# Slots of five row terms for the sampling weights, and two ScalarE copies per step in place of four

## The chip, the cores and the metric

The kernel runs on one core of a Trainium2 chip. The metric is the time of one execution on the device, in microseconds; the median of three runs of the kernel before is 2926.32 us.

## The reference, cut to what matters

The input is 32 samples of 64 channels of 56 x 56. Two residual parts follow one another. The first normalises groups, takes signs, and runs two grouped 3 x 3 convolutions with batch normalisation. The second is a deformable convolution, and the change lies in it alone:

```python
x = x + _L0_conv_ref(_gn(x), ...)
x = x + _L1_conv_ref(_gn(x), ...)

def _L1_conv_ref(x, dw_w, dw_b, om_w, om_b, vp_w, vp_b, op_w):
    value = (xf @ vp_w.T + vp_b).reshape(n, L, G, cg)           # G = 8 groups of 8 channels
    om_in = depthwise_3x3(x, dw_w) + dw_b
    om = om_in @ om_w.T + om_b                                  # 8 x 9 taps x (dy, dx, mask)
    py, px = pixel + tap + offset
    sampled = bilinear(value, py, px)                           # four neighbours, weights from the fractions
    out = einsum('nhwgk,nhwgkc->nhwgc', mask, sampled)
    return out.reshape(n, L, c) @ op_w.T
```

As long as every offset lies within one pixel, the sum over taps and neighbours touches a window of 5 x 5 pixels around the output pixel. The kernel uses that: it forms 25 window weights per pixel and group and applies them as matrix products. Other offsets raise a flag, and a general part after it does the work again; in these runs it is skipped.

## The kernel before, in words

The program has three parts: the two passes of the first block (`l0_passes`), the deformable block (`l1_pass`, line 739), and the skipped general part. The change is in `l1_pass`. It works on 16 pairs of samples, and cuts each image into 14 bands of 4 rows; one band of a pair is a step, so there are 224 steps (i is the pair, j the band). The lanes are 64 positions of a row for each of two samples.

Each engine has its own list of work per step, written out by hand, and the engines are tied by semaphores. Work for one band is spread over several steps:

- ScalarE: `hats` of step + 2 (five instructions, L1119 to L1125), every second step `copy_acc` (L1157), `copy_weights` (L1135), every second step `write_weights` (L1149, a DMA from its own queue), `taps` of step + 5 (nine products of the depthwise convolution, L1109).
- GpSimd (POOL): `merge` of step + 1 (L1062, L1065), `depthwise` of step + 4 (L1048 to L1055).
- TensorE: `apply` (L1280), `windows` (L1258), then `offsets_and_misc` (L1195, L1200, and `project`, L1207).
- VectorE: `copy_om` of step + 2 (L960, out of PSUM with the bias), `mask_hats` and `products` of step + 1 (L969, L979), in 7 of 14 steps sums for the next pair (`sum_half`, L920 to L927), and `read_misc` (L986, L952).
- SyncE issues the DMAs: values out to DRAM and back into `vbd`, window weights from DRAM into `abuf`, images in and out.

TensorE's `offsets_and_misc` waits for `read_misc` of the step before, for POOL's `depthwise` and for VectorE's `copy_om`; `copy_om` waits for the offsets of the step before; `windows` waits for POOL's `merge` and for the last `copy_weights`.

The path of the window weights is what the change touches. `copy_om` leaves the 27 x 8 offsets and masks of four rows in `oms`, with the order of the 32 values per tap as (half of the groups, row, group). `products` and `merge` keep that order in `pr`. `windows` shifts and adds them with nine matmuls per step into `win_p`, five shifts e of 160 columns, each in a place of 172 columns; a float32 matmul leaves two records in the trace. `copy_weights` spreads them into `wst` with one ScalarE instruction per row k of the band:

```python
for k in range(BR):
    to = 2 * BR * (2 - 2 * (k % 2)) + BR * u + k
```

In `wst`, a slot has 6 x 16 elements (`PC` = 96) and a lane's band 5 slots (`BAND` = 480). Two bands (u = 0, 1) share a slot. An odd row's five terms sit one place lower than an even row's, so that two rows that are neighbours can be read side by side; six places are therefore kept, and the sixth of each is zero. Every second step the whole of `wst` goes to DRAM in a skewed layout, and 14 DMAs bring it back into `abuf` so that lanes become source pixels.

`apply` multiplies the values of each source row yq (`vbd`, 32 columns of weights) with `abuf`. It takes the output rows that yq reaches, up to five, rounded outwards to pairs of rows, since pairs lie next to one another in `abuf`. Four matmuls (two samples, two halves b) stand side by side in four column tiles of the array. One half of the image width is done in even steps (34 columns, 128 lanes), the other in odd steps (26 columns, 96 lanes).

Of the kernel before, what the change touches and what calls it, by code (L numbers as in the profile page):

```python
# [30 lines left out]
S = 2  # L31
HH = H // 2
HALF = HH * W
TAPS = 9
# [10 lines left out]
G = 8  # L45
GK = G * TAPS
OMC = 3 * GK
LANES = 128
BR = 4
NT = H // BR  # L50
TN = BR * W
# [6 lines left out]
GS = 4  # L58
CT = 5
RT = 5  # L60
RP = RT + 1
WP = 172
PC = 2 * BR * RP * 2
BAND = CT * PC
PX = 4
SEEN = (PX + CT - 1) * PC
LINE = GS * SEEN + PC
QB = 36
QC = 64
VSLOT = 7  # L70
TP = 2 * W
TILES = HW // TP
# [6 lines left out]
def wait(eng, sem, value):  # L79

    if not isinstance(value, int) or value > 0:
        eng.wait_ge(sem, value)
# [656 lines left out]
def l1_pass(nc, ab3, flag, kept, w_d, v_d, out, pairs):  # L739
# [4 lines left out]
    with ctx:  # L744
        def sb(name, shape, dt=f32):
            return ctx.enter_context(nc.sbuf_tensor(name, shape, dt))
# [4 lines left out]
        def pm(name, cols):  # L751
            return ctx.enter_context(nc.psum_tensor(name, [128, cols], f32))

        N = NT * pairs
        cst, wts, ombt, vbt, smat, y, x3h = (
            kept.cst, kept.wts, kept.ombt, kept.vbt, kept.smat, kept.y, kept.x3h)
        l2h, xp, omin, vbd, eps, minus1, far = (
            kept.l2h, kept.xp, kept.omin, kept.vbd, kept.eps, kept.minus1, kept.far)
        dwt = sb("dwt", [128, 2, TAPS, TN])
        oms = sb("oms", [LANES, 2, 3 * TAPS, BR * G])  # L760
        ht = sb("ht", [LANES, 2, 3, 2 * TAPS, BR * G])
        pr = sb("pr", [LANES, 2, 11, 3, 3, BR * G])
        wst = sb("wst", [LANES, GS, BAND])
        abuf = sb("abuf", [128, S, QC * PC])
        vsb = sb("vsb", [LANES, 2, GS, G, BR * 2])
        accs = sb("accs", [128, 2, TN])
        bn3 = sb("bn3", [128, 2 * PIECES, BN_F])
# [4 lines left out]
        om_p = pm("om_p", 2 * BANK)  # L772
        win_p = pm("win_p", 2 * BANK)
        acc_p = pm("acc_p", BANK)
# [55 lines left out]
        with nc.Block() as block:  # L830
            @block.sync
            def _(sp):
# [14 lines left out]
                def read_weights(i, j, half):  # L847
# [5 lines left out]
                    for m in range(READS[half]):  # L853
                        seen = bass.AP(lines.tensor, lines.offset + (32 * half + PX * m) * LINE,
                                       [[SEEN, GS * PX], [XL * LINE, S], [1, SEEN]])
                        at = (QB * half + PX * m) * PC
                        sp.dma_start(abuf[GS * PX * m:GS * PX * (m + 1), :, at:at + SEEN], seen).then_inc(a_in[half], 16)

# [55 lines left out]
            def _(dve):  # L914
# [43 lines left out]
                def copy_om(i, j):  # L958
                    dve.wait_ge(om_ready, NT * i + j + 1)
                    dve.tensor_tensor(  # L960
                        oms[:, j % 2, :, :].rearrange("q w (b k g) -> q (w b) k g", b=2, g=GS),
                        om_p[:, :].rearrange("q (k z) -> q k z", k=BR)[:, :, 0:OMC].rearrange("q k (v g) -> q v k g", g=GS),
                        ombt[:, :].rearrange("q (v g) -> q v g", g=GS).unsqueeze(2).broadcast_to([LANES, 6 * TAPS, BR, GS]),
                        ALU.add).then_inc(om_ok, 1)

                def mask_hats(i, j):
# [53 lines left out]
                for j in range(2):  # L1020
                    copy_om(0, j)
# [70 lines left out]
            def _(act):  # L1092
# [34 lines left out]
                def copy_weights(i, j):  # L1127
                    t, u = NT * i + j, j % 2
                    if u == 0:
                        wait(act, w_out, 16 * (t // 2))  # L1130
                    act.wait_ge(win_ok, t + 1)
                    for k in range(BR):
                        to = 2 * BR * (2 - 2 * (k % 2)) + BR * u + k
                        cells = wst[:, 0, to:to + 1]
                        ins = act.activation(  # L1135
                            bass.AP(cells.tensor, cells.offset, [cells.ap[0], [PC, CT], [2 * BR, 2 * RT], [BAND, GS]]),
                            win_p[:, 0:CT * WP].rearrange("p (e z) -> p e z", e=CT)[:, :, 0:RT * BR * G].rearrange(
                                "p e (m k g) -> p e m k g", k=BR, g=GS)[:, :, :, k, :],
                            ACT.Copy)
                    ins.then_inc(wst_ok, 1)  # L1140

                def write_weights(i, j):
# [3 lines left out]
                    for half in range(2):  # L1146
                        wait(act, a_in[half], 16 * READS[half] * (D - 1))
                    lines = w_d[D % 2, :].rearrange("(l z) -> l z", z=LINE)[:, 0:GS * SEEN].rearrange("l (g q) -> l g q", q=SEEN)
                    act.dma_start(lines[:, :, 0:BAND], wst[:, :, :]).then_inc(w_out, 16)  # L1149

# [35 lines left out]
            def _(pe):  # L1186
# [63 lines left out]
                def windows(i, j):  # L1250
                    t = NT * i + j
                    wait(pe, wst_ok, t)
                    pe.wait_ge(mg_ok, t + 1)
                    for e in range(CT):
                        terms = [(a, b) for a in range(3) for b in range(3) if 2 - (a + b - 2) == e]
                        to = WP * e
                        for n, (a, b) in enumerate(terms):
                            mm = pe.matmul(win_p[:, to:to + 160], smat[:, e, :],  # L1258
                                           pr[:, j % 2, 0:RT, a, b, :],
                                           start=n == 0, stop=n == len(terms) - 1)  # L1260
                    mm.then_inc(win_ok, 1)

                def apply(i, j, half):

                    D, y0 = (NT * i + j) // 2, BR * j
                    pe.wait_ge(a_in[half], 16 * READS[half] * (D + 1))
                    if half == 0:
                        for b in range(j + 1 if j else 0, min(j + 3, NT)):
                            pe.wait_ge(vb_in[b % VSLOT], 4 * 16 * (2 * i + b // VSLOT + 1))
                        wait(pe, accs_ok, D)  # L1270
                    qb, K, x0, x1 = ((0, 128, 0, 34), (1, 96, 30, W))[half]
                    rows = range(max(0, y0 - 2), min(H, y0 + 2 * BR + 2))
                    for yq in rows:
                        t0, t1 = max(0, yq - y0 - 2) // 2, min(2 * BR - 1, yq - y0 + 2) // 2
                        for s in range(S):
                            for b in range(2):
                                seen = abuf[0:K, s, :]
                                at = (QB * qb + x0 - 32 * qb + 2) * PC + 4 * BR * (y0 + 2 * t0 - yq + 3) + 2 * BR * b + 2 * t0
                                mov = bass.AP(seen.tensor, seen.offset + at, [seen.ap[0], [8 * BR + 2, t1 - t0 + 1], [PC, x1 - x0], [1, 2]])
                                mm = pe.matmul(  # L1280
                                    acc_p[32 * (2 * s + b):32 * (2 * s + b) + 32, 0:2 * TN].rearrange("p (t w r) -> p t w r", t=BR, r=2)[:, t0:t1 + 1, x0:x1, :],
                                    vbd[0:K, 1 - s, qb, yq // BR % VSLOT, :, :, 2 * (yq % BR) + b].rearrange("p g c -> p (g c)"),
                                    mov, start=yq == rows[0] and qb == 0, stop=yq == rows[-1] and qb == 1,
                                    skip_group_check=True)
                    mm.then_inc(amat_ok, 1)

                def step(i, j, first, last):
# [15 lines left out]
                for j in range(LAG):  # L1303
                    if j < 4:
                        apply(pairs - 1, NT - 4 + j // 2 * 2, j % 2)
                    offsets_and_misc(N + j + 3, output=(pairs - 1, NT + j - LAG))
# [275 lines left out]
def program(nc, x, w1t, w2t, par, con, con3, wts3, omb, vpb, places, out):  # L1582

    samples = x.shape[0]
    pairs = samples // S
    l1_d = nc.dram_tensor("l1_scratch", [pairs, 128, HALF], f32).ap()
    l2_d = nc.dram_tensor("l2_scratch", [pairs, S * CO, HW], f32).ap()
    x3_d = nc.dram_tensor("x3_scratch", [samples, C, HW], f32).ap()
    w_d = nc.dram_tensor("weight_scratch", [2, LANES * LINE], f32).ap()
    v_d = nc.dram_tensor("rows_scratch", [2, LANES * BR * C], f32).ap()  # L1590
    vpad = nc.dram_tensor("value_scratch", [G * VP * VP, C // G], f32).ap()
    with nc.sbuf_tensor("ab3", [128, 2], f32) as ab3, nc.sbuf_tensor("flag", [1, 1], i32) as flag:
        with ExitStack() as ctx:
            kept = Kept(nc, ctx, x, x3_d, l2_d, con3, wts3, omb, vpb, pairs)
            l0_passes(nc, x, w1t, w2t, par, con, l1_d, l2_d, x3_d, ab3, kept, pairs)
            l1_pass(nc, ab3, flag, kept, w_d, v_d, out, pairs)
        l2_s = l2_d.rearrange("q (s c) f -> (q s) c f", s=S)
        general_pass(nc, x, x3_d, l2_s, ab3, flag, con3, wts3, omb, vpb, places, vpad, out, samples)
# [66 lines left out]
```

## Time and profile before

| | us |
|---|---|
| median of 3 runs | 2926.32 |
| lowest, highest of the runs | 2924.11, 2930.4 |
| the profiled execution | 2924.83 |
| its span, from the first to the last instruction | 2923.0 |
| PE busy (matmuls) | 2430.8 |
| PE weight loads busy | 2021.2 |
| DVE busy | 2205.6 |
| ACT busy | 2259.7 |
| POOL busy | 1917.6 |

The span covers all parts of the program; the deformable block begins after some 700 us. Busy times are sums over the whole span, and a matmul's end is modelled, so a busy TensorE need not be at its peak. The waits name what ended an engine's idle time, as far as the profile shows it; "issue" stands where it shows nothing. The mean time of an instruction counts its latency, and successive ones overlap, so busy time by count is shorter.

### The profile page before, as it was taken

The numbers are of one execution on the slowest core, as the hardware profiler recorded it, in microseconds if no ns is written. First come the engines' busy times: TensorE is split into PE (matmuls) and PEld (weight loads), VectorE is DVE, ScalarE is ACT, GpSimd is POOL, SyncE is SP. The second block draws the span as 40 slices with busy tenths as digits, with TensorE's granted clock in tenths as the row PEclk, the third lists the DMA queues.
The fourth block names the chain that finished last, engine by engine and source line by source line (L and its number), as shares of the span: only waits on it lengthen the run. The fifth ranks groups of instructions, "written<-read, shape, count | busy, mean of one in ns | idle before, by whom it ended". The sixth has DMA issues, their size and how long they took to land. (4 is left out here: it accounts for less than half of the span.)

```text
span 2923.0 us, 100581 instructions
## 1 busy us (share of the span) xinstructions
PE 2430.8 (83%) x40456; PEld 2021.2 (69%) x40456; DVE 2205.6 (75%) x3095; ACT 2259.7 (77%) x4721; POOL 1917.6 (66%) x1452
## 2 busy tenths in 40 slices
PE   3999779993688888888888888888888888888887
PEld 2666556772577777777777777777777777777786
DVE  3555423334989897989888898989898988989773
ACT  2444256662989889898989898898989898989892
POOL 1000000003888888888988888888988898988892
PEclk8999889996899999999999999999999999999998
DMA  4555579975577677777777777777778777877675
GB/s 103 130 132 144 143 182 265 263 199 172 124 191 203 181 195 192 188 191 190 204 194 192 187 200 195 197 183 193 199 189 198 188 196 187 206 179 190 177 176 147
DMA packets 356164, 538.18 MB, mean 184 GB/s; under 512 B 171728, under 2 KB 258256, under 8 KB 355536
## 3 DMA queue, kind: packets, MB, share of 16 engines
q1 hardware_dynamic: 296656, 422.71, 60.3%
q10 hardware_dynamic: 59136, 110.11, 10.8%
q8 instruction: 283, 4.64, 0.8%
q14 instruction: 89, 0.73, 0.1%
HBM read 312.82 MB, written 219.77 MB: 182 GB/s over the span
## 5 line engine op out<-in xcount | busy, mean ns | idle before, releaser
L1109 ACT ACTIVATE dwt<-xp,wts 128x224 f32<-128x224 f32 x2016 | 797.3, 484 | 40.8 <-ACT wst L1135 31.8
L1280 PE MATMUL acc_p<-abuf,vbd 128*32 128x136 f32 (+5 forms) x20480 | 710.4, 291 | 54.9 <-issue 46.0
L1280 PEld LDWEIGHTS acc_p<-abuf,vbd 128*32 128x32 f32 (+1 forms) x20480 | 645.9, 145 | 117.7 <-issue 60.5
L979 DVE TENSOR_TENSOR pr<-mh_p,ht 128x864 f32<-128x864 f32 x672 | 668.9, 1051 | 23.2
L1258 PE MATMUL win_p<-pr,smat 128*128 128x160 f32 x4032 | 626.7, 310 | 27.3 <-POOL pr L1065 15.8
L246 PE MATMUL cv<-cin,wb 128*64 128x392 bf16 x6912 | 590.4, 333 | 25.8 <-ACT cin L225 25.8
L1258 PEld LDWEIGHTS win_p<-pr,smat 128*128 128x128 f32 x4032 | 570.4, 194 | 51.2 <-issue 22.4
L246 PEld LDWEIGHTS cv<-cin,wb 128*64 128x64 bf16 x6912 | 401.4, 110 | 208.7 <-ACT cin L225 25.9
L1048 POOL TENSOR_TENSOR dwt<-dwt 128x896 f32<-128x896 f32 x224 | 516.3, 2305 | 4.7 <-ACT dwt L1109 4.7
L1062 POOL TENSOR_TENSOR pr<-pr 128x576 f32<-128x576 f32 x224 | 317.3, 1417 | 187.8 <-DVE pr L979 187.8
L1135 ACT ACTIVATE wst<-win_p 128x200 f32<-128x200 f32 x896 | 388.6, 605 | 62.4 <-PE win_p L1258 38.7
L969 DVE TENSOR_TENSOR mh_p<-oms,ht 128x864 f32<-128x864 f32 x224 | 408.8, 1825 | 8.5 <-ACT ht L1125 8.5
L1200 PE MATMUL om_p<-wts,omin 64*64 64x216 f32 x3584 | 406.4, 369 | 10.2 <-POOL omin L1055 10.2
L1195 PE MATMUL misc<-wts,xp 64*64 64x64 f32 x3584 | 181.6, 234 | 265.7 <-issue 214.3
L1195 PEld LDWEIGHTS misc<-wts,xp 64*64 64x64 f32 x3584 | 149.8, 137 | 311.2 <-issue 310.7
L1065 POOL TENSOR_TENSOR pr<-pr 128x576 f32<-128x576 f32 x224 | 338.7, 1512 | 31.2
L1050 POOL TENSOR_TENSOR dwt<-dwt 128x448 f32<-128x448 f32 x224 | 336.5, 1502 | 17.6
L1200 PEld LDWEIGHTS om_p<-wts,omin 64*64 64x64 f32 x3584 | 246.1, 139 | 47.8 <-issue 11.6
L986 DVE TENSOR_TENSOR y<-y,misc 128x224 f32 (+1 forms) x224 | 85.2, 380 | 248.2 <-PE misc L1207 247.5
L253 ACT ACTIVATE lt<-cv 128x392 f32<-128x392 f32 x128 | 60.9, 492 | 265.9 <-PE cv L246 265.5
L960 DVE TENSOR_TENSOR oms<-om_p,ombt 128x864 f32<-128x864 f32 x224 | 238.2, 1063 | 10.1 <-PE om_p L1200 10.1
L1119 ACT ACTIVATE ht<-oms 128x576 f32<-128x576 f32 x224 | 151.2, 675 | 102.7 <-DVE oms L960 102.4
(132 smaller groups left out, 2674.9 us busy)
## 6 DMA issues: line engine op xcount, KB each, us to landing
abuf<-weight_scratch SPq DMA_DIRECT2D x1568, 96.0 KB, 3.3
weight_scratch<-wst ACTq DMA_DIRECT2D x112, 960.0 KB, 6.2
xt<-x SPq DMA_DIRECT2D x128, 392.0 KB, 7.6
rows_scratch<-vsb SPq DMA_DIRECT2D x224, 128.0 KB, 2.1
vbd<-rows_scratch SPq DMA_DIRECT2D x896, 32.0 KB, 3.2
x_scratch<-xt SPq DMA_DIRECT2D x64, 392.0 KB, 6.6
y<-x SPq DMA_DIRECT2D x64, 392.0 KB, 4.4
x3h<-x_scratch SPq DMA_DIRECT2D x64, 392.0 KB, 4.9
```

Of the source, the lines that this page charges most:

```text
L246: mm = pe.matmul(cv[c][64 * h:64 * h + 64, 0:CN], wb[:, layer, j, k, :], cin[:, u, r:r + CR, k % 3:k % 3 + W], start=(k == 0 and j == 0), ...
L969: dve.tensor_tensor(mh[:, :, :, :], oms[:, j % 2, 2 * TAPS:3 * TAPS, :].unsqueeze(1).broadcast_to([LANES, 3, TAPS, BR * G]), ht[:, j % 2, ...
L979: dve.tensor_tensor(pr[:, j % 2, slots, :, :, :].rearrange("p k e x z -> p e k (x z)"), mh[:, a, :, :].rearrange("p (k x) z -> p k (x z)", ...
L1048: pool.tensor_tensor(d[:, 0:4, :], d[:, 0:4, :], d[:, 4:8, :], ALU.add).then_inc(dw1_ok, 1)
L1050: pool.tensor_tensor(d[:, 0:2, :], d[:, 0:2, :], d[:, 2:4, :], ALU.add).then_inc(dw2_ok, 1)
L1065: pool.tensor_tensor(rows(slice(1, 3)), rows(slice(1, 3)), rows(slice(5, 11, 5)), ALU.add).then_inc(mg_ok, 1)
L1109: ins = act.activation(dwt[:, j % 2, k, :].rearrange("p (r w) -> p r w", w=W), image[:, r:r + BR, k % 3:k % 3 + W], ACT.Identity, scale=dw ...
L1135: ins = act.activation(bass.AP(cells.tensor, cells.offset, [cells.ap[0], [PC, CT], [2 * BR, 2 * RT], [BAND, GS]]), win_p[:, 0:CT * WP].rea ...
L1195: return pe.matmul(misc[64 - 64 * s:128 - 64 * s, to:to + C], xp[64 * s:64 * s + 64, at:at + XL], vpw[64 * s:64 * s + 64, :], start=True, ...
L1200: return pe.matmul(om_p[64 * s:64 * s + 64, 256 * r:256 * r + OMC], omin[64 * s:64 * s + 64, j % 2, r, :], omw[64 * s:64 * s + 64, :], sta ...
L1258: mm = pe.matmul(win_p[:, to:to + 160], smat[:, e, :], pr[:, j % 2, 0:RT, a, b, :], start=n == 0, stop=n == len(terms) - 1)
L1280: mm = pe.matmul(acc_p[32 * (2 * s + b):32 * (2 * s + b) + 32, 0:2 * TN].rearrange("p (t w r) -> p t w r", t=BR, r=2)[:, t0:t1 + 1, x0:x1, :],
```

## The change

A slot gets five places of 16 elements (`PC` = 80). An odd row's first term, which lay in the place that only odd rows used, now lies in the last place of the slot before it, which odd rows leave free; one more place ends a band (`BAND` = 416). `SEEN`, `LINE`, `QB`, `QC` and the size of `abuf` follow from that.

`copy_weights` writes with one instruction per parity r of the row. It takes two rows k of the same parity as its innermost pair, 8 bytes apart in `wst`, and 400 elements. For the source to be read at an even step, the order of the 32 values per tap becomes (group, row): `copy_om` reads `om_p` with the four rows innermost, which lie 256 elements apart in PSUM, and still writes `oms` without a gap. `win_p` loses its padding; its fourth shift now crosses the end of a bank of 512 columns, and its matmuls are cut into 32 and 128 columns.

In `apply`, pairs can no longer be padded with zeros at the ends, since the neighbouring place holds another slot's term. A source row is applied in up to three runs: an odd first row alone, the pairs, and an even last row alone.

```diff
-RP = RT + 1
-WP = 172
-PC = 2 * BR * RP * 2
-BAND = CT * PC
+RW = 4 * BR
+PC = RT * RW
+BAND = CT * PC + RW
 PX = 4
-SEEN = (PX + CT - 1) * PC
+SEEN = (PX - 1) * PC + BAND
 LINE = GS * SEEN + PC
-QB = 36
-QC = 64
+QB = 37
+QC = 65
...
-        abuf = sb("abuf", [128, S, QC * PC])
+        abuf = sb("abuf", [128, S, QC * PC + RW])
...
                     dve.tensor_tensor(
-                        oms[:, j % 2, :, :].rearrange("q w (b k g) -> q (w b) k g", b=2, g=GS),
-                        om_p[:, :].rearrange("q (k z) -> q k z", k=BR)[:, :, 0:OMC].rearrange("q k (v g) -> q v k g", g=GS),
-                        ombt[:, :].rearrange("q (v g) -> q v g", g=GS).unsqueeze(2).broadcast_to([LANES, 6 * TAPS, BR, GS]),
+                        oms[:, j % 2, :, :].rearrange("q w (g k) -> q (w g) k", k=BR),
+                        om_p[:, :].rearrange("q (k z) -> q z k", k=BR)[:, 0:OMC, :],
+                        ombt[:, :].unsqueeze(2).broadcast_to([LANES, OMC, BR]),
                         ALU.add).then_inc(om_ok, 1)
...
-                    for k in range(BR):
-                        to = 2 * BR * (2 - 2 * (k % 2)) + BR * u + k
+                    for r in range(2):
+                        to = RW * (1 - r) + BR * u + r
                         cells = wst[:, 0, to:to + 1]
                         ins = act.activation(
-                            bass.AP(cells.tensor, cells.offset, [cells.ap[0], [PC, CT], [2 * BR, 2 * RT], [BAND, GS]]),
-                            win_p[:, 0:CT * WP].rearrange("p (e z) -> p e z", e=CT)[:, :, 0:RT * BR * G].rearrange(
-                                "p e (m k g) -> p e m k g", k=BR, g=GS)[:, :, :, k, :],
+                            bass.AP(cells.tensor, cells.offset, [cells.ap[0], [2 * BR, 2 * CT * RT], [BAND, GS], [2, 2]]),
+                            win_p[:, 0:CT * RT * BR * G].rearrange("p (m g k r) -> p r m g k", g=GS, k=2, r=2)[:, r],
                             ACT.Copy)
...
-                        to = WP * e
+                        cuts = (0, 1, RT) if e == 3 else (0, RT)
                         for n, (a, b) in enumerate(terms):
-                            mm = pe.matmul(win_p[:, to:to + 160], smat[:, e, :],
-                                           pr[:, j % 2, 0:RT, a, b, :],
-                                           start=n == 0, stop=n == len(terms) - 1)
+                            for m0, m1 in zip(cuts, cuts[1:]):
+                                mm = pe.matmul(win_p[:, BR * G * (RT * e + m0):BR * G * (RT * e + m1)], smat[:, e, :],
+                                               pr[:, j % 2, m0:m1, a, b, :],
+                                               start=n == 0, stop=n == len(terms) - 1)
...
-                        t0, t1 = max(0, yq - y0 - 2) // 2, min(2 * BR - 1, yq - y0 + 2) // 2
...
+                        k0, k1 = max(0, yq - y0 - 2), min(2 * BR - 1, yq - y0 + 2)
+                        t0, t1 = (k0 + 1) // 2, (k1 + 1) // 2
+                        runs = (((k0, 1, 1),) if k0 % 2 else ()) + (((2 * t0, t1 - t0, 2),) if t1 > t0 else ()) + (
+                            ((k1, 1, 1),) if k1 % 2 == 0 else ())
+                        for ka, n, r in runs:
...
+                                    row = y0 + ka - yq + 3 - ka % 2
+                                    at = (QB * qb + x0 - 32 * qb + 2) * PC + RW * row + 2 * BR * b + ka
+                                    mov = bass.AP(seen.tensor, seen.offset + at, [seen.ap[0], [2 * RW + 2, n], [PC, x1 - x0], [1, r]])
+                                    mm = pe.matmul(
+                                        acc_p[32 * (2 * s + b):32 * (2 * s + b) + 32, 0:2 * TN].rearrange("p (t w r) -> p t w r", t=BR, r=2)[
+                                            :, ka // 2:ka // 2 + n, x0:x1, ka % 2:ka % 2 + r],
```

## Rows read from the trace of the kernel before

**Rows 1.** Busy time by stretch, 1200 to 2800 us: from:to, length, engines, PEclk, DMA share, GB/s

```profile
core 0: us, PE busy (x) PEld busy (x) DVE busy (x) ACT busy (x) POOL busy (x), PEclk, DMA share, GB/s
1200.00:2800.00 1600.00, 1345.38 (x24810) 1186.20 (x24804) 1416.43 (x1800) 1436.87 (x3273) 1390.53 (x1031) 0.97 0.76 191
```

**Rows 2.** Groups by line, same stretch, DVE: xcount | busy us, mean ns | idle before

```profile
L960 DVE TENSOR_TENSOR oms<-om_p,ombt 128x864 f32<-128x864 f32 x166 | 176.5, 1063 | 0.0
...
L952 DVE TENSOR_TENSOR vsb<-misc,vbt 128x128 f32<-128x128 f32 x332 | 112.2, 430 | 0.0
...
L986 DVE TENSOR_TENSOR y<-y,misc 128x224 f32 (+1 forms) x166 | 63.1, 380 | 153.9 <-PE misc L1207 153.3
```

**Rows 3.** Waits, same stretch: engine, line, waited for: us, times, longest

```profile
PE misc L1195 <- issue: 161.9, 113, 3.0
DVE y L986 <- PE misc L1207: 153.3, 75, 5.9
POOL pr L1062 <- DVE pr L979: 134.8, 87, 6.1
ACT ht L1119 <- DVE oms L960: 78.1, 32, 6.3
...
PE misc L1195 <- DVE oms L960: 35.2, 12, 4.5
...
ACT wst L1135 <- DMA weight_scratch<-wst: 17.7, 15, 2.1
...
PE misc L1207 <- ACT accs L1157: 7.8, 12, 1.2
```

**Rows 4.** Timeline, 1717 to 1731 us: start, length, instruction, [idle before]

```profile
1725.81 2.99 DVE L979 TENSOR_TENSOR pr<-mh_p,ht 128x864 f32<-128x864 f32 x3
...
1726.36 0.66 POOL L1055 TENSOR_TENSOR omin<-dwt 128x224 f32<-128x224 f32 x1
...
1727.23 0.27 PE L1195 MATMUL misc<-wts,xp 64*64 64x64 f32 x2 [2.11 <-issue]
...
1727.91 1.41 POOL L1062 TENSOR_TENSOR pr<-pr 128x576 f32<-128x576 f32 x1 [0.89 <-DVE pr L979]
...
1728.76 0.59 PE L1207 MATMUL misc<-accs,wts 64*64 64x112 f32 x8
...
1729.50 0.39 DVE L986 TENSOR_TENSOR y<-y,misc 128x224 f32 x1 [0.70 <-PE misc L1207]
...
1730.31 1.06 DVE L960 TENSOR_TENSOR oms<-om_p,ombt 128x864 f32<-128x864 f32 x1
```

**Rows 5.** Groups by line, whole span, ACT

```profile
L1135 ACT ACTIVATE wst<-win_p 128x200 f32<-128x200 f32 x896 | 388.6, 605 | 62.4 <-PE win_p L1258 38.7 <-DMA weight_scratch<-wst 23.5
...
L1119 ACT ACTIVATE ht<-oms 128x576 f32<-128x576 f32 x224 | 151.2, 675 | 102.7 <-DVE oms L960 102.4
...
L225 ACT ACTIVATE cin<-xt 64x1568 bf16 (+1 forms) x64 | 96.8, 1512 | 2.0
...
L253 ACT ACTIVATE lt<-cv 128x392 f32<-128x392 f32 x128 | 60.9, 492 | 265.9 <-PE cv L246 265.5
L1157 ACT ACTIVATE accs<-acc_p 128x448 f32<-128x448 f32 x112 | 59.0, 527 | 27.2 <-PE acc_p L1280 27.1
```

**Rows 6.** Groups by line, whole span, PE

```profile
L1280 PE MATMUL acc_p<-abuf,vbd 128*32 128x136 f32 (+5 forms) x20480 | 710.4, 291 | 54.9 <-issue 46.0 <-DMA abuf<-weight_scratch 8.6
...
L1189 PE MATMUL misc<-rh,cst 128*128 128x2 f32 x32 | 7.9, 317 | 17.9 <-DVE rh L937 17.9
```

**Rows 7.** Timeline of PE, four blocks of matmuls in different steps

```profile
1729.28 2.55 PE L1280 MATMUL acc_p<-abuf,vbd 96*32 96x104 f32 x80
...
1781.12 3.42 PE L1280 MATMUL acc_p<-abuf,vbd 128*32 128x68 f32 x96
...
2017.98 2.79 PE L1280 MATMUL acc_p<-abuf,vbd 96*32 96x52 f32 x96
2020.70 2.71 PE L1258 MATMUL win_p<-pr,smat 128*128 128x160 f32 x18
```

**Rows 8.** DMA queues of the page: packets, MB, share of 16 engines

```profile
q8 instruction: 283, 4.64, 0.8%
```

More of the change, by code:

```diff
@@ L1273, in apply @@
                     for yq in rows:
-                        t0, t1 = max(0, yq - y0 - 2) // 2, min(2 * BR - 1, yq - y0 + 2) // 2
[L1275 to L1284, printed above, removed]
+                        k0, k1 = max(0, yq - y0 - 2), min(2 * BR - 1, yq - y0 + 2)
@@ new lines, in apply @@
+                        t0, t1 = (k0 + 1) // 2, (k1 + 1) // 2
+                        runs = (((k0, 1, 1),) if k0 % 2 else ()) + (((2 * t0, t1 - t0, 2),) if t1 > t0 else ()) + (
+                            ((k1, 1, 1),) if k1 % 2 == 0 else ())
+                        for ka, n, r in runs:
+                            opens = qb == 0 and yq == rows[0] and ka == k0
+                            for s in range(S):
+                                for b in range(2):
+                                    seen = abuf[0:K, s, :]
+                                    row = y0 + ka - yq + 3 - ka % 2
[4 more added lines that the diff above has]
+                                            :, ka // 2:ka // 2 + n, x0:x1, ka % 2:ka % 2 + r],
+                                        vbd[0:K, 1 - s, qb, yq // BR % VSLOT, :, :, 2 * (yq % BR) + b].rearrange("p g c -> p (g c)"),
+                                        mov, start=opens, stop=yq == rows[-1] and qb == 1 and ka == runs[-1][0],
+                                        skip_group_check=True)
```

## The prediction

> **What bounds the kernel now.** I read the busy times of the steady stretch first, then who waited for whom in it, then one turn of the loop in the timeline, then the rows that price single instructions.
>
> Between 1200 and 2800 us no engine is full: ACT 1437, DVE 1416, POOL 1391 and PE 1345 us of 1600 [rows 1]. The third part runs 166 of its 224 steps there, one `copy_om` (L960) each [rows 2], so a step takes 1600 / 166 = 9.64 us. A loop sets the pace, and the waits show which [rows 3]. POOL waits 134.8 us for DVE's products. DVE waits 153.3 us for PE's `misc`. PE waits 161.9 us ahead of `misc`, in 113 steps, put down to "issue". The timeline tells what that is [rows 4]: POOL's `omin` ends at 1726.36 + 0.66 = 1727.02, and PE, idle for 2.11 us, starts at 1727.23. So it is DVE products, POOL merge and depthwise, PE offsets and `misc`, DVE addition and `copy_om`, and round again. `copy_om` (L960) stands in that loop; the ScalarE copies do not. ACT is the busiest engine, but what others wait for on it in 1600 us is 7.8 us of `accs` [rows 3].
>
> **The change part by part.**
>
> *ScalarE copies.* ACT's slope from the two SBUF rows is (1512 - 675) / (1568 - 576) = 0.844 ns per element, so a copy out of PSUM has 492 - 392 x 0.844 = 161 ns fixed [rows 5]. `accs` reads PSUM at a step of two elements and fits that: 161 + 378 = 539 against 527. The old copy, 200 elements in 605 ns, pays (605 - 161) / 200 = 2.22 ns per element: the price is in the write, where each element lands 1920 bytes from the last. Four of them cost 4 x 434 (388.6 / 896) = 1.74 us per step, successive ones overlapping by 605 - 434 = 171 ns. A new copy of 400 writes two cells 8 bytes apart, then jumps. Low end, no jump is paid: 499 ns each, 0.83 us for two with the overlap. High end, every element is still paid: 1049 ns, 1.93 us. If two share a jump, 1.53 ns each, it is 1.38 us. I take 1.1, between the low end and the shared jump: 0.63 us saved, 141 us of ACT over 224 steps. The Trainium skill, in Advanced Engine Details and Errata, section Memory Cachelines, says that SBUF lines are 16 bytes and that two hits on a line absorb its latency; by that it would be the low end, 0.83. No row here has two hits per line.
>
> What of it reaches the end is bounded by the waits on ACT: 7.8 us in 1600, so 7.8 x 224 / 166 = 11 us. I take -10. Below that nothing waits; a ScalarE that is done earlier waits longer for `oms` (78.1 us already, in 32 steps [rows 3]).
>
> *`copy_om`.* Same count, same contiguous write, but its PSUM read now takes four elements 1 KB apart before it moves on, where it took four neighbours. DVE's rows: slope (1063 - 380) / (864 - 224) = 1.07 ns per element, 140 ns fixed [rows 2]. It already runs at that slope, so there is nothing to gain. Upper end: what DVE pays for a scattered SBUF write, `vsb`, (430 - 140) / 128 = 2.27 ns per element; 864 at that price are 2.10 us, 1.04 us more per step, on the loop. I take 0: the nearest row, ACT's `accs`, steps over every second PSUM element and pays nothing [rows 5]. The upper end is the first rival.
>
> *Windows on PE.* Their outputs now stand without padding, so the fourth shift would cross column 512 (the code's BANK), and its two terms are cut into 32 and 128 columns: 22 matmul records per step for 18. Columns are the same. Low end: 0. High end: the row with short matmuls on 128 x 128 weights, L1189, 7.9 / 32 = 247 ns each [rows 6], so 4 x 0.25 = 1.0 us. 18 records of 160 columns take 2.71 us [rows 7], 0.15 each; a 32-column record streams a fifth of that but still loads all 128 weight columns. I take 0.075 us for each added one, 0.30 per step, nearer to the stream than to L1189, whose matmuls wait for nothing behind them.
>
> *Apply on PE.* Before: 12 source rows inside an image, each as one run of one to three row pairs for four side-by-side tiles, two passes: 96 records per half. After, odd ends are runs of one row: 8 single rows, 4 single pairs, 6 double pairs, 18 runs, 144 records; columns fall from 48 to 40 rows' worth. In the 26-wide half, 96 records take 2.79 us and 80, without two one-pair runs, 2.55 [rows 7]: 0.24 / 4 = 60 ns per pass of a single pair. Less a last matmul's 0.25 us, 2.54 - 8 x 0.060 = 2.06 us are left for 40 pairs in longer runs, 51 ns each. After: 8 x 60 + 24 x 51 + 16 singles. A single costs 26 ns if only columns count and 60 if the pass has a floor: 2.12 to 2.66 us, -0.42 to +0.12. The 34-wide half (3.42 us), worked alike with 66 ns a pair, gives -0.5 to 0. I take the upper ends, since a lone pair of 52 columns is dearer than one in a run: +0.06 per step on average. A single also writes every second PSUM element; twice the column price, 52, is still under the 60.
>
> *Instructions.* PE's matmul records go from 40456 to 52104 (20480 x 122 / 80 in apply, 4032 x 22 / 18 in windows). Instructions come by DMA, 283 packets [rows 8]; PE's idle time put down to issue inside apply is 46.0 us [rows 6]. If it grows with apply's records, +52%, that is 24 us.
>
> *PE on the path.* (0.30 + 0.06) x 224 + 24 = 105 us. PE waits ahead of `misc` in 113 + 12 of 166 steps [rows 3]; in the other 41, a quarter, added work delays `misc`. In 7 of 14 steps DVE is then still busy with the next image's sums. 105 x 0.25 x 0.5 = 13 us; at least 0, at most 26.
>
> *DMA, SP, POOL.* A slot is 320 bytes for 384, so the weight write falls from 960 to 832 KB and each read from 96 to 82. Counts and queues stay. The one wait it eases is ACT's 17.7 us for the write [rows 3], and ACT is off the loop: 0. SP gets no new wait. POOL's clears shrink before the loop starts: 0.
>
> **Sum.** -10 + 13 + 0 = +3 on the profiled 2924.83 us, whose span is 2923.0; that execution is 1.5 us under the median of the runs, so the forecast is 2929 us. About 0.2%, 6 us, is what a measurement can tell from no change.
>
> **The rivals.**
>
> 1. *`copy_om` pays for its scattered PSUM read.* Slower. 1.04 us more on the loop's one DVE entry, with ACT's hats, DVE's mask and PE's next offsets queued behind it. DVE waits for `misc` in 75 of 166 steps [rows 3]; if those hid it, 0.55 x 224 x 1.04 = 128 us would remain, if none did, 233. As the wait itself is a return of the same loop I take 150: 3076 us. It decides once an element costs more than some 0.05 ns extra. For it: DVE does pay double for scattered writes. Against: `accs`. Chance 0.22. The Trainium skill, same section, gives PSUM lines of 8 bytes and says "Every two consecutive elements should be contiguous for best throughput", which would make this rival true; by the same rule `accs`, one element per line, should be slow, and it is not.
>
> 2. *PE becomes the bound.* Lone rows above the 60 ns, windows near 1 us, or instruction fetch that no longer keeps up with shorter instructions; with 1.3 us more per step PE's 1345 us become 1560 of 1600. Half of the excess over its waits, some 25 us, shows: 2952 us. For it: the idle times at issue. Against: 161.9 us of waiting. Chance 0.17.
>
> 3. *ACT sets the pace after all.* It waits for `oms` in 32 and for PE in a few of 166 steps and runs through in most. If taps that come 0.63 us earlier pull POOL's depthwise forward in a third of the steps, 0.33 x 224 x 0.63 = 47, some 35 after what PE gives back: 2891 us. Against: POOL shows no wait for taps in the stretch. Chance 0.14.
>
> 4. *The copies do not get cheaper.* The jump is paid per element, 1.93 us for 1.74; ACT loses 0.2 per step and some of its slack: 2933 us. Chance 0.05.
>
> **How the numbers follow.** The forecast has 0.42, with a range of its own of 2912 to 2945: of it 0.08 lies under 2920, 0.24 within 6 us, 0.10 above. Faster: 0.08 + 0.14 = 0.22. Same: 0.24 + 0.02 + 0.03 from rivals 2 and 4 = 0.29. Slower: 0.10 + 0.22 + 0.15 + 0.02 = 0.49. The range for 8 in 10 reaches from rival 3, 2890, to rival 1, 3085; it leaves out rival 1's upper end.
>
> **What the new profile would show.** L1135's successor at some 600 to 700 ns for 400 elements, two per step; `copy_om` at 1.06 us (2.1 makes rival 1); windows near 3.0 us per step and apply within 0.2 of 2.8 and 3.4 us; DVE's wait for `misc` near 150 us, ACT's for `oms` well above 78.1. I am wrong on the loop if ACT's waits stay small while the time falls, and on PE if its wait ahead of `misc` vanishes.

## The result and the profile after

The changed kernel takes 2987.86 us (median of 4 runs, 2986.08 to 2995.11) against 2925.22 us for the kernel before on the same chip: ratio 1.022, 95% interval 1.0193 to 1.0246. It is slower by some 63 us; whether by more or less than 2%, the interval leaves open. The profiled execution took 2987.32 us, its span 2985.5. The granted clock is 0.945 over its span and was 0.952 before. It is not what is looked for: a run below with 0.931 takes about as long (2991.37 us, though with fewer columns), and the same instructions in another order, also below, keep PE busy for 2534.6 us at 0.953, only 11 us less than here (2545.8).

First the pace. In 1200 to 2800 us, busy time by stretch and VectorE's group `copy_om` of the changed kernel, the answers to [rows 1, 2]:

```profile
1200.00:2800.00 1600.00, 1384.18 (x32182) 1250.44 (x32175) 1351.88 (x1754) 1282.15 (x2838) 1328.44 (x994) 0.95 0.60 170
```

```profile
L959 DVE TENSOR_TENSOR oms<-om_p,ombt 128x864 f32<-128x864 f32 x160 | 171.8, 1074 | 0.0
```

160 steps stand where 166 stood: 10.0 us each for 9.64. Six steps of 9.64 us are 58 us lost in this stretch, known to about one step. No engine is full: PE has 1384 of 1600 us, only 39 more than before. So it is not PE's busy time that became the bound. The waits of the same stretch, which answer to [rows 3]:

```profile
DVE y L985 <- PE misc L1205: 217.2, 73, 7.3
POOL pr L1061 <- DVE pr L978: 199.7, 105, 5.3
...
ACT wst L1134 <- PE win_p L1257: 130.2, 61, 5.3
PE acc_p L1285 <- issue: 128.6, 82, 4.5
ACT ht L1118 <- DVE oms L959: 126.9, 49, 6.2
...
PE misc L1193 <- issue: 56.9, 56, 2.5
```

and two rows of the kernel before, same view, that weren't shown:

```profile
PE acc_p L1280 <- issue: 38.0, 32, 3.2
...
ACT wst L1135 <- PE win_p L1258: 21.7, 14, 4.3
```

Everybody now waits longer for PE: VectorE for `misc` (153.3 to 217.2 us), ScalarE for the windows (21.7 to 130.2), and POOL behind VectorE (134.8 to 199.7). PE itself waits much less for the others (ahead of `misc` 161.9 to 56.9 us). It stands still inside `apply`, where no other engine and no data hold it: 38.0 to 128.6 us. The groups by line over the whole span, against [rows 2, 5, 6]:

```profile
L1257 PE MATMUL win_p<-pr,smat 128*128 128x160 f32 (+2 forms) x4928 | 755.5, 313 | 33.3 <-issue 20.0 <-POOL pr L1064 13.3
L1285 PE MATMUL acc_p<-abuf,vbd 128*32 128x34 f32 (+5 forms) x31232 | 726.7, 251 | 177.3 <-issue 173.1 <-DMA abuf<-weight_scratch 4.2
...
L959 DVE TENSOR_TENSOR oms<-om_p,ombt 128x864 f32<-128x864 f32 x224 | 240.2, 1072 | 11.6 <-PE om_p L1198 11.6
L1134 ACT ACTIVATE wst<-win_p 128x400 f32<-128x400 f32 x448 | 216.8, 543 | 205.9 <-PE win_p L1257 194.8 <-DMA weight_scratch<-wst 10.5
```

The copies do what the change wants: two of 543 ns for four of 605. `copy_om` is unchanged. `apply` is busy 16 us longer, and idle at issue 173.1 us for 46.0: 127 us more. In the timeline of PE such a pause looks like this (the last two rows are a step without one):

```profile
2005.17 2.68 PE L1285 MATMUL acc_p<-abuf,vbd 96*32 96x26 f32 x128
2008.91 0.45 PE L1285 MATMUL acc_p<-abuf,vbd 96*32 96x52 f32 x16 [1.07 <-issue]
```

```profile
1723.87 2.91 PE L1285 MATMUL acc_p<-abuf,vbd 96*32 96x26 f32 x144
1726.71 3.06 PE L1257 MATMUL win_p<-pr,smat 128*128 128x160 f32 x22
```

`apply` has no wait on a semaphore between its 1st and 144th record. The queue of [rows 8] grew in step:

```profile
q8 instruction: 374, 6.13, 0.9%
```

That is 91 packets more. A matmul record has a weight load beside it, so PE has 2 x (52104 - 40456) = 23296 instructions more: 256 per added packet. I numbered PE's instructions in the order of the trace (a record two, with its load; the sequencer's own one each) and took every pause of over 450 ns between two loads of one line after 1000 us. All 111 of the changed kernel stand at number 156 or 157 modulo 256; so do all 46 of the kernel before. And between 1200 and 2800 us such a pause ends 1.3 to 1.6 us after the end of an instruction packet's transfer (10th to 90th percentile; before 1.3 to 1.7). PE stands at the border of two packets and waits for the second one. The Trainium skill has this in Advanced Engine Details and Errata, section ISA Cache: a line holds 256 instructions, and there are two lines. (The same lines give TensorE 128 KB, which at 16 KB a line would be eight.) The trace agrees with 256 instructions, 16 KB a packet, and with one line in hand while the next one comes: none of the 254 packets of this stretch sets out more than 294 instructions ahead of its border. Their median is 143 instructions ahead, but the 93 that PE then waits for have a median of 80; before it was 42 of 197 packets, with a median of 80 as well. Busier DMA engines are not the reason: their share fell from 0.76 [rows 1] to 0.60.

### The profile page after: what moved, and what is told of

It reads as the page before. It is cut to its first block and busy times, and to the rows that moved or that the text cites. A ratio compares the mean times of both kernels' runs of the same rounds, so it can differ in the third digit from the quotient of the medians.

```text
span 2985.5 us, 123429 instructions
## 1 busy us (share of the span) xinstructions
PE 2545.8 (85%) x52104; PEld 2169.7 (73%) x52104; DVE 2172.3 (73%) x3095; ACT 2112.7 (71%) x4273; POOL 1899.9 (64%) x1452
## 5 line engine op out<-in xcount | busy, mean ns | idle before, releaser
L1285 PE MATMUL acc_p<-abuf,vbd 128*32 128x34 f32 (+5 forms) x31232 | 726.7, 251 | 177.3 <-issue 173.1
L1285 PEld LDWEIGHTS acc_p<-abuf,vbd 128*32 128x32 f32 (+1 forms) x31232 | 680.6, 155 | 227.0 <-issue 191.9
L1257 PE MATMUL win_p<-pr,smat 128*128 128x160 f32 (+2 forms) x4928 | 755.5, 313 | 33.3 <-issue 20.0
L1257 PEld LDWEIGHTS win_p<-pr,smat 128*128 128x128 f32 x4928 | 699.1, 206 | 49.5 <-issue 25.7
L1198 PE MATMUL om_p<-wts,omin 64*64 64x216 f32 x3584 | 393.9, 361 | 8.7 <-POOL omin L1054 8.6
L968 DVE TENSOR_TENSOR mh_p<-oms,ht 128x864 f32<-128x864 f32 x224 | 375.3, 1675 | 7.1 <-ACT ht L1124 7.1
L1134 ACT ACTIVATE wst<-win_p 128x400 f32<-128x400 f32 x448 | 216.8, 543 | 205.9 <-PE win_p L1257 194.8
L1049 POOL TENSOR_TENSOR dwt<-dwt 128x448 f32<-128x448 f32 x224 | 321.3, 1434 | 17.6
L1198 PEld LDWEIGHTS om_p<-wts,omin 64*64 64x64 f32 x3584 | 239.6, 137 | 44.9 <-issue 10.6
L959 DVE TENSOR_TENSOR oms<-om_p,ombt 128x864 f32<-128x864 f32 x224 | 240.2, 1072 | 11.6 <-PE om_p L1198 11.6
```

The lines of the kernel that those rows point to most:

```text
L968: dve.tensor_tensor(mh[:, :, :, :], oms[:, j % 2, 2 * TAPS:3 * TAPS, :].unsqueeze(1).broadcast_to([LANES, 3, TAPS, BR * G]), ht[:, j % 2, ...
L1049: pool.tensor_tensor(d[:, 0:2, :], d[:, 0:2, :], d[:, 2:4, :], ALU.add).then_inc(dw2_ok, 1)
L1198: return pe.matmul(om_p[64 * s:64 * s + 64, 256 * r:256 * r + OMC], omin[64 * s:64 * s + 64, j % 2, r, :], omw[64 * s:64 * s + 64, :], sta ...
L1257: mm = pe.matmul(win_p[:, BR * G * (RT * e + m0):BR * G * (RT * e + m1)], smat[:, e, :], pr[:, j % 2, m0:m1, a, b, :], start=n == 0, stop= ...
L1285: mm = pe.matmul(acc_p[32 * (2 * s + b):32 * (2 * s + b) + 32, 0:2 * TN].rearrange("p (t w r) -> p t w r", t=BR, r=2)[:, ka // 2:ka // 2 + ...
```

## The experiments

Theory A: the split runs of `apply` ask for instructions faster than they come, and the pauses are the loss. 288 instructions in 2.91 us are 10.1 ns each, so a packet's 256 last 2.6 us, where they lasted 3.7 (192 in 2.79 us [rows 7]). From a packet's start to the end of a pause go 2.3 to 2.9 us (10th to 90th percentile; before 2.4 to 3.3). Rivals: B, the four added window matmuls; C, the slots and their reads; D, the lone rows' own columns.

**The split alone, on the old slots.**

```diff
-    t0, t1 = max(0, yq - y0 - 2) // 2, min(2 * BR - 1, yq - y0 + 2) // 2
...
+    for ka, n, r in runs:
...
+    at = (QB * qb + x0 - 32 * qb + 2) * PC + 4 * BR * (y0 + ka - ka % 2 - yq + 3) + 2 * BR * b + ka
```

> The kernel before with nothing changed but apply, which issues the same runs as the changed kernel (odd ends of a source row as runs of one row, 144 matmul records per half for 96) on the old six-place slots. Theory A (more and shorter matmuls in apply outrun the supply of PE's instructions): idle at issue inside apply rises from 46 us to 150 to 190 over the whole span, and the time from 2925 to 2970 to 2990 us. Rival B (the four added window matmuls are what costs): at most 2940 us. Rival C (the five-place slots, their reads at other addresses and the later reads of them): 2925 to 2935 us.

2996.74 us, ratio 1.0237 (1.0206 to 1.0267). `apply` of that kernel, groups by line:

```profile
L1285 PE MATMUL acc_p<-abuf,vbd 128*32 128x34 f32 (+5 forms) x31232 | 771.3, 260 | 186.3 <-issue 178.7 <-DMA abuf<-weight_scratch 7.2
```

The split alone brings the whole loss, with the pauses (178.7 us) that were expected; the time is 7 us above the expected range. As causes of the loss, B and C fall.

**All but the split.**

```diff
-    for ka, n, r in runs:
...
+    t0, t1 = max(0, yq - y0 - 2) // 2, min(2 * BR - 1, yq - y0 + 2) // 2
+    at = (QB * qb + x0 - 32 * qb + 2) * PC + RW * (y0 + 2 * t0 - yq + 3) + 2 * BR * b + 2 * t0
```

> The changed kernel with apply's runs as before (whole row pairs, 96 records per half) on the five-place slots; the odd end of a run then reads the neighbour of its pair, which belongs to another slot, so apply's sums are not the reference's. Everything else of the change stays: copies, copy_om order, cut windows, smaller slots. Theory A: 2910 to 2935 us, idle at issue inside apply back at 40 to 60 us over the span. Rival B or C: 2960 us or more.

2917.51 us, ratio 0.9969 (0.9957 to 0.9982):

```profile
L1279 PE MATMUL acc_p<-abuf,vbd 128*32 128x136 f32 (+5 forms) x20480 | 658.1, 280 | 52.6 <-issue 48.4 <-DMA abuf<-weight_scratch 3.7
...
L1134 ACT ACTIVATE wst<-win_p 128x400 f32<-128x400 f32 x448 | 215.7, 540 | 99.4 <-PE win_p L1257 90.2 <-DMA weight_scratch<-wst 8.4
```

The pauses are back at 48.4 us and the rest of the change is worth some 10 us to the good. The busy time of 658.1 us for the same records that took 710.4 [rows 6] is taken up below.

**Count or columns.**

```diff
     for ka, n, r in runs:
+        xe = x1 if r == 2 else x0 + 2
...
```

(`xe` then takes the place of `x1` in what is read and in what is written.)

> The changed kernel with the runs of one row cut to 2 of their 26 or 34 columns (that work is left out); the count of matmuls stays. Theory A (count of instructions): 2970 to 2995 us, idle at issue inside apply 160 to 230 us, since PE asks for instructions sooner still. Rival D (the lone rows' own columns, with every second PSUM element written, are what costs): 2935 us or less.

2991.37 us, ratio 1.0218 (1.0196 to 1.024); waits in 1200 to 2800 us:

```profile
PE acc_p L1286 <- issue: 129.1, 66, 4.1
```

With 2 columns for 26 or 34 in every lone row the kernel takes as long as the changed one. D falls: it is the count of instructions. This is the run with the granted clock of 0.931.

**The windows' cut alone.**

```diff
+    cuts = (0, 1, RT) if e == 3 else (0, RT)
+    for m0, m1 in zip(cuts, cuts[1:]):
         for n, (a, b) in enumerate(terms):
-            mm = pe.matmul(win_p[:, to:to + 160], ...)
+            mm = pe.matmul(win_p[:, WP * e + BR * G * m0:WP * e + BR * G * m1], ...)
```

> The kernel before with the fourth shift's windows cut into 32 and 128 columns, as in the changed kernel, and nothing else: 22 matmul records per step for 18. Windows take 3.0 to 3.1 us per step for 2.71. Theory A: that alone is small beside the loss, 2926 to 2940 us, with the idle time at issue inside apply within 15 us of the 38 in 1200 to 2800 us. Rival B: 2960 us or more.

2935.61 us, ratio 1.0033 (1.0017 to 1.0048), some 9.5 us. The two parts of the cut run one after the other here, where the changed kernel alternates them. `apply`, groups by line:

```profile
L1281 PE MATMUL acc_p<-abuf,vbd 128*32 128x136 f32 (+5 forms) x20480 | 703.3, 289 | 54.1 <-issue 43.9 <-DMA abuf<-weight_scratch 9.9
```

Idle time at issue in `apply` is about as before. So the cut has a small price of its own, inside the expected range, and B is excluded a second time.

**The copies alone.** The old slots can take two copies, with the loops in another order and `copy_om` as it was:

```diff
-    for k in range(BR):
-        to = 2 * BR * (2 - 2 * (k % 2)) + BR * u + k
+    for r in range(2):
+        to = 4 * BR * (1 - r) + BR * u + r
...
+            bass.AP(cells.tensor, cells.offset, [cells.ap[0], [BAND, GS], [PC, CT], [2 * BR, 2 * RT], [2, 2]]),
+            bass.AP(taken.tensor, taken.offset, [taken.ap[0], [1, GS], [WP, CT], [4 * GS, 2 * RT], [2 * GS, 2]]),
```

> The kernel before with nothing changed but the ScalarE copies: two of 400 elements that write neighbours, on the old six-place slots, with windows, apply and copy_om as they were. If the write alone decides (theory A takes it so), a copy takes 500 to 560 ns although it now reads PSUM at a step of eight elements, two per step of the loop; the time is 2905 to 2925 us, since PE's instructions are what they were. If the copies' earlier end were itself harmful (rival E: other cores' work of the loop collides with earlier windows), 2940 us or more.

2934.71 us, ratio 1.0025 (1.0014 to 1.0036): slower, against theory A's 2905 to 2925, and short of rival E's 2940. Groups by line:

```profile
L1279 PE MATMUL acc_p<-abuf,vbd 128*32 128x136 f32 (+5 forms) x20480 | 702.4, 290 | 73.5 <-issue 66.9 <-DMA abuf<-weight_scratch 6.4
...
L1257 PE MATMUL win_p<-pr,smat 128*128 128x160 f32 x4032 | 645.0, 316 | 42.9 <-issue 26.0 <-POOL pr L1065 16.8
...
L1135 ACT ACTIVATE wst<-win_p 128x400 f32<-128x400 f32 x448 | 211.6, 530 | 122.6 <-PE win_p L1257 107.9 <-DMA weight_scratch<-wst 14.3
```

The windows of the kernel before, same view:

```profile
L1258 PE MATMUL win_p<-pr,smat 128*128 128x160 f32 x4032 | 626.7, 310 | 27.3 <-POOL pr L1065 15.8 <-issue 10.7 <-ACT wst L1135 0.6
```

The copy is as cheap as expected, but with PE's program unchanged its pauses grew (46.0 to 66.9 us in `apply`, 10.7 to 26.0 in the windows). Why they grew is open. It is tempting to say that PE's idle time ahead of `misc` let the next packet come, and that a faster ScalarE shortens it; the trace does not bear that out. Between 1200 and 2800 us, 1 of the 197 packets of the kernel before sets out while PE waits there (197 us; 24 packets by share of time), and 0 of 196 with the copies alone (174 us). If the pauses ate the gain, it must appear once they are gone.

**The same instructions in another order.** Eight of the twelve source rows, then the windows, then the other four; first on the changed kernel, then on the kernel before, then on the copies alone:

```diff
-    for yq in rows:
+    for yq in (rows[0:8], rows[8:])[part]:
...
-    apply(*n, j % 2)
+    apply(*n, j % 2, 0)
     windows(i, j)
+    if n:
+        apply(*n, j % 2, 1)
```

> The changed kernel with the order of PE's work alone altered: eight of apply's source rows, then the windows, then the other four rows, and the offsets after them. Every instruction stays, so 374 instruction packets stay. Theory A, put as density (288 instructions in some 2.9 us are asked for faster than one packet of 256 comes, 2.3 to 2.9 us; the windows' 44 slow ones in between let the next packet arrive): idle at issue inside apply falls from 177 us over the span to under 70, the time to 2925 to 2955 us. Rival F (each added packet costs, wherever it falls): 2975 to 2995 us. Against both: accs are ready later, so PE may wait for them ahead of the projection, up to 1 us in every second step.

> The kernel before with the same reordering (eight source rows, windows, four rows) and nothing else. By theory A it had 46 us of such idle time inside apply over the span; if that shrinks to under 20 and the wait for accs stays small, 2895 to 2925 us. If what PE waits for ahead of misc is what sets the pace and the idle time lay beside it, 2920 to 2932 us. If the later accs cost more than the supply gives back, 2940 us or more.

> The kernel with the copies alone (two of 400, old slots, old runs) and the same reordering. The copies alone came out 7 us slower than before while the idle time at issue inside apply rose by some 17 us in the 1600 us looked at; by theory A the reordering takes that away and leaves the copies' gain: 2885 to 2920 us, below both others. If the copies cost something of their own, it stays 5 us or more above the kernel before with the reordering.

| us (ratio, interval) | old order | eight and four |
|---|---|---|
| changed kernel | 2987.86 (1.022) | 2934.06 (1.0023, 1.0011 to 1.0036) |
| kernel before | 1 | 2915.45 (0.996, 0.9945 to 0.9975) |
| copies alone | 2934.71 (1.0025) | 2908.65 (0.9936, 0.9914 to 0.9959) |

`apply` in the three, groups by line, in this order (one fence per kernel):

```profile
L1286 PE MATMUL acc_p<-abuf,vbd 128*32 128x34 f32 (+5 forms) x31232 | 754.4, 252 | 73.6 <-issue 54.1 <-DMA abuf<-weight_scratch 19.3
```

```profile
L1281 PE MATMUL acc_p<-abuf,vbd 128*32 128x136 f32 (+5 forms) x20480 | 742.5, 292 | 29.5 <-DMA abuf<-weight_scratch 29.0
```

```profile
L1280 PE MATMUL acc_p<-abuf,vbd 128*32 128x136 f32 (+5 forms) x20480 | 744.7, 292 | 24.4 <-DMA abuf<-weight_scratch 23.3 <-issue 0.8
```

The changed kernel gives back 54 of its 63 us with 374 packets as before, so F (each packet costs, wherever it falls) is wrong: by theory A, what costs is that they are wanted in a bunch. The kernel before gives back about 11 us of time with its 46.0 us of pauses. And with the pauses gone the copies alone are 6.8 us faster than the kernel without them, where they had been 7 us slower: the gain is real, and the old order hid it. The new order does a second thing, though. ScalarE gets its windows sooner, and waits 34.5 us for them in the changed kernel where it waited 194.8:

```profile
L1134 ACT ACTIVATE wst<-win_p 128x400 f32<-128x400 f32 x448 | 215.0, 540 | 34.7 <-PE win_p L1257 34.5
```

That is rival G below, and no reordered run has the one without the other.

**Six and six, and windows first.** `rows[0:6]` and `rows[6:]` on the changed kernel and on the copies alone; `rows[0:0]` and all of `rows` on the changed kernel.

> The changed kernel with apply's source rows in two halves of six around the windows, where eight and four left 54 us of idle time at issue inside apply over the span. Theory A (density: at most 144 apply instructions, 1.5 us, come one after the other for 192, 2 us): under 25 us of it, and 2910 to 2928 us, on a level with or below the kernel before. If the remaining loss is the 12 longer bursts' place and not their length, or the later accs cost as much, it stays at 2930 us or more.

> The copies alone with six and six rows for eight and four. With eight and four its idle time at issue inside apply was 0.8 us, so theory A has nothing left to give: 2904 to 2914 us, at most 4 us from the 2908.65. Later accs would show as 2915 us or more.

> The changed kernel with the windows wholly ahead of apply, so that the ScalarE copies get theirs sooner still but all 288 instructions of apply stand together. Theory A (the density of apply is what costs): idle at issue inside apply stays at 100 us or more over the span and the time at 2960 us or more. Rival G (what the reordering mended is that windows came too late for ScalarE): 2940 us or less whatever the idle time is. PE may also wait for POOL's merge ahead of the windows, up to 2 us per step, which apply covered before; a high time with a low idle time at issue would be that and would tell nothing.

The changed kernel comes to 2918.14 us (0.9958, 0.9944 to 0.9973), its pauses in `apply` to 12.1 us (first fence); the copies alone to 2903.79 us (0.9917, 0.9901 to 0.9934), a little below what was expected and the fastest version here. The second fence has ScalarE's copies in that one, and what they wait for:

```profile
L1286 PE MATMUL acc_p<-abuf,vbd 128*32 128x136 f32 (+5 forms) x31232 | 752.1, 252 | 41.5 <-DMA abuf<-weight_scratch 28.5 <-issue 12.1
```

```profile
L1135 ACT ACTIVATE wst<-win_p 128x400 f32<-128x400 f32 x448 | 209.5, 526 | 9.7 <-DMA weight_scratch<-wst 5.8 <-PE win_p L1257 3.9
```

With the windows wholly ahead the changed kernel took 2939.32 us (1.0035, 1.0022 to 1.0049). Theory A's expectation of it was wrong, and by its letter G's (2940 us or less) came true. PE's groups there:

```profile
L1257 PE MATMUL win_p<-pr,smat 128*128 128x160 f32 (+2 forms) x4928 | 718.2, 304 | 210.4 <-POOL pr L1064 182.8 <-DMA abuf<-weight_scratch 25.5 <-ACT wst L1134 1.0
L1286 PE MATMUL acc_p<-abuf,vbd 128*32 128x34 f32 (+5 forms) x31232 | 696.5, 249 | 23.4 <-issue 18.0 <-DMA abuf<-weight_scratch 4.5
```

288 instructions stand together, and yet the pauses are 18.0 us, not 100. So the density of `apply` by itself does not decide; what goes before it counts. Here 44 slow instructions (3.03 us) and a wait for POOL's merge go before, and when a packet sets out some 120 or more instructions of the one before it are still to be done in nine of ten cases; in the changed kernel one packet in ten has 2 or fewer. That is counted from the trace, but which of the two, the slow matmuls or the wait, gives the packet its lead was not taken apart; only 1 of 261 packets sets out during that wait. Nor does this run tell A from G, since its pauses went as well. Against G as the whole account stands the kernel with whole runs: ScalarE waits 90.2 us for windows there, for 38.7 before [rows 5], and yet it is 10 us faster, though its copies are shorter too. That the split costs, and that PE's added idle time lies at the borders of packets, is shown; how much of what the new order gives back is due to the packets, and how much to the earlier windows, is not.

## Why the prediction was wrong

The forecast of 2929 us (own range 2912 to 2945) was wrong; the second rival happened, in the third of its forms, at more than twice its price (63 us for some 25). "Slower" had the largest chance, and the range for 8 in 10 holds the result, but that is luck: the upper part of the range and 0.22 of the 0.49 were there for the first rival, which is false.

- **The step that failed** is the term for instructions, "If it grows with apply's records, +52%, that is 24 us". Measured: +127 us, 46.0 to 173.1. The idle time does not grow with the records. A pause is what a packet takes less what the instructions in hand last, and inside `apply` 256 of them last 2.6 us for 3.7. The packets that PE waits for set out with some 80 instructions in hand; those last 0.8 us for 1.2 before (10.1 for 14.5 ns each), and a packet takes 2.3 to 2.9. In the stretch the pauses inside `apply` are longer, 1.6 us for 1.2 on average, and above all more, 82 for 32; what decides when a packet sets out, and so how many are late, no run explains. The packets were there [rows 8], and so were the times per block [rows 7]; I divided neither by the other, and did not ask how long a packet takes.
- **PE on the path** ("105 x 0.25 x 0.5 = 13 us") failed with it. Half of the added idle time reached the end: 63 us of 127, about the share that I gave to rival 2 and not to the forecast. (Rival 2's "some 25" is for the 1600 us; over 224 steps it would be 36.) The cover, the waits ahead of `misc` in 125 of 166 steps, was largely used up: 61 of 160 are left.
- **The rival's reason against itself**, "161.9 us of waiting", didn't hold: 105 of these went.
- **ScalarE copies**: predicted 1.1 us per step with a low end of 0.83; two take 216.8 / 224 = 0.97. The overlap of 171 ns was taken off four times for the old copies and once for the new pair; taken off twice, the low end is 0.66, the shared jump 1.20, and rival 4 pays 1.76 for 1.74. The Trainium skill's rule on two hits per line (Advanced Engine Details and Errata, section Memory Cachelines), which was named for the low end, is nearly borne out: 543 ns for 400 elements where 200 took 605, that is 0.96 ns per element above the 161 ns for 2.22 before, where SBUF rows give 0.844. What reaches the end was put at 10 us; it measures 6.8 with the pauses gone (2915.45 to 2908.65) and -7 with them.
- **`copy_om`**: 1072 ns for 1063. Right; the first rival, which had the larger chance, is false for this read. The Trainium skill's sentence on PSUM pairs (same page and section), which the prediction took to make it true, stands there beside one on matmuls; for this VectorE read it is not borne out.
- **Windows**: +0.30 us per step predicted; 3.06 for 2.71 measured. By the prediction's own factors that is 0.30 x 224 x 0.125 = 8.4 us, and the cut alone cost 9.5. Right.
- **Apply's busy time**: +0.06 per step (13 us) predicted, +16 us measured, by two errors that cancel. Single undisturbed blocks in the timeline, first of the split on old slots, then of whole runs on new slots:

```profile
1824.09 3.04 PE L1285 MATMUL acc_p<-abuf,vbd 96*32 96x26 f32 x144
...
1850.79 3.53 PE L1285 MATMUL acc_p<-abuf,vbd 128*32 128x34 f32 x144
```

```profile
1825.66 2.59 PE L1279 MATMUL acc_p<-abuf,vbd 96*32 96x52 f32 x96
...
1952.30 3.15 PE L1279 MATMUL acc_p<-abuf,vbd 128*32 128x68 f32 x96
```

The medians of all blocks without a gap (no matmul starts over 250 ns after the last), at a granted clock of 1, are 2.78 and 3.43 us before, 3.05 and 3.57 with the split, 2.62 and 3.18 on the new slots: the split costs 0.27 and 0.14 us, the new slots save 0.16 and 0.25.
- **DMA**: 0, and ScalarE's wait for the write was to ease: 17.7 to 8.2 us in the stretch. Nothing of the loss lies there.

The sign named for an error on PE ("if its wait ahead of `misc` vanishes") is what the waits show.

## What to carry to other kernels

Where an engine's program is unrolled, count its instructions per microsecond in the densest stretch and hold that against the rate at which its packets come, before costing an edit by columns: here 256 instructions in 2.6 us were too many and in 3.7 us mostly not. It is a warning and not a rule: with the windows wholly ahead the same dense block had few pauses. Idle time at issue inside a block without semaphores is the sign, and a changed order (slow matmuls between the fast ones) took it away here without one instruction less. An edit that is worth little may be hiding behind such pauses, and should be tried again once they are gone.

## What was not expected of the hardware

- Every pause of PE inside a block stands at a border of 256 instructions (111 of 111, 46 of 46). The same program of PE had 66.9 us of them in `apply` for 46.0 once the copies were cheaper.
- While PE waits for other engines, hardly any instruction packet sets out: ahead of `misc`, 1 of 197 in 197 us before, 0 of 254 in 67 us in the changed kernel, where the share of time would make it 24 and 11. So such a wait helps only a packet that is already under way.
- The same matmuls on `abuf` ran 6 to 7% faster with slots 320 bytes apart than with 384 (medians 2.62 for 2.78 us, 3.18 for 3.43). The copies alone and the cut alone leave them at 2.78 and 3.42. What does it, the size of the step, where it falls in memory, or the smaller DMA traffic beside it, was not tried.
- ScalarE reads PSUM at a step of eight elements no slower than at a step of two: 530 ns for 400 in the copies alone, 543 in the changed kernel, where pairs are two apart.
